# A product-key expert search in which one 128-wide tail search per head replaces two 64-wide ones

## What is computed

```python
h = dct(frames(x))                         # (32, 313, 128)
h = h + attention(layernorm(h))
hid = layernorm(h)
q = layernorm_heads(hid @ Wq.T + bq)       # 8 heads x 64, two halves of 32
s0 = l2norm(q[..., :32]) @ l2norm(keys0).T # 64 scores per head and half
s1 = l2norm(q[..., 32:]) @ l2norm(keys1).T
sc0, ix0 = top_k(s0, 16)
sc1, ix1 = top_k(s1, 16)
cs = sc0[..., :, None] + sc1[..., None, :] # 16 x 16 candidates
ci = ix0[..., :, None] + ix1[..., None, :] # the expert of a candidate (0 to 126)
fs, pos = top_k(cs, 16)
w = softmax(fs)
out = h + sum over heads and picks of gelu(hid . down[fi]) * w * up[fi]
```

## Time and profile before

| | |
|---|---|
| median of 3 runs | 2107.41 us (2103.27 to 2129.34) |
| the profiled execution | 2100.36 us |
| its span (first to last instruction) | 2098.2 us |
| DVE busy | 1929.6 us (92%) |
| PE busy | 1694.7 us (81%) |
| POOL busy | 1634.6 us (78%) |
| ACT busy | 1215.4 us (58%) |
| DMA engines busy | 10% or less in every slice |

### The profile page before, as it was taken

The page is one execution under the profiler, slowest core; times in us unless marked ns, Lnnn a source line. Parts: engine busy times, 40 slices in busy tenths (PEclk is TensorE's granted clock), DMA queues, the critical chain, the costliest instruction groups (busy, mean ns, idle before and its releaser), DMA issues.

```text
span 2098.2 us, 48149 instructions
## 1 busy us (share of the span) xinstructions
PE 1694.7 (81%) x10975; PEld 1316.2 (63%) x10975; DVE 1929.6 (92%) x15878; ACT 1215.4 (58%) x3835; POOL 1634.6 (78%) x3523
## 2 busy tenths in 40 slices
PE   5567898878889887887888788788878988888666
PEld 3335576765767676575767667676766766566555
DVE  3299999999999999999999999999999999999992
ACT  3345655566565566666566666656666566665454
POOL 2238787897878788787878878787887878888785
PEclk9676767778776777887677788767877677776655
DMA  1000000000000000000000000000000000000000
GB/s 35 12 10 2 19 7 7 19 9 18 6 19 7 6 19 9 19 7 19 7 6 18 9 19 7 19 6 6 19 9 19 7 13 13 6 13 9 6 8 9
DMA packets 46676, 24.86 MB, mean 12 GB/s; under 512 B 4955, under 2 KB 46116, under 8 KB 46390
## 3 DMA queue, kind: packets, MB, share of 16 engines
q1 hardware_dynamic: 46390, 21.80, 3.7%
HBM read 11.52 MB, written 10.26 MB: 10 GB/s over the span
## 4 chain that ended last, share of the span: by engine, by line
PE 38%; DVE 30%; POOL 13%; ACT 12%; issue 7%; SPq 0%; another core or an unknown queue 0%; DMA 0%; ACTq 0%; DVEq 0%; POOLq 0%
PE QB L529 7%; DVE alpha L1050 5%; PE FB L447 5%; PE FB L438 5%; PE SC L481 4%; DVE idx L1034 4%; DVE idx L1037 4%; DVE hrest L1028 3%; PE QB L517 3%; PE FB L419 3%; ACT WD L729 3%; POOL sa L759 3%; ACT hi L669 3%; PE FB L427 3%; DVE vals L1032 2%
## 5 line engine op out<-in xcount | busy, mean ns | idle before, releaser
L529 PE MATMUL QB<-bw,alpha 128*128 128x48 bf16 x5120 | 553.8, 277 | 58.0 <-issue 56.8
L529 PEld LDWEIGHTS QB<-bw,alpha 128*128 128x128 bf16 x5120 | 522.1, 151 | 95.5 <-issue 85.9
L896 POOL TENSOR_TENSOR bw<-beta,wp 128x1024 bf16<-128x1024 bf16 x240 | 504.1, 2130 | 96.9 <-ACT wp L715 96.9
L729 ACT ACTIVATE WD<-QB 32x96 f32<-32x96 f32 x1280 | 307.5, 240 | 78.5 <-PE QB L529 67.3
L481 PE MATMUL SC<-WK,hidT 128*128 128x512 f32 x320 | 238.5, 837 | 54.2 <-ACT stdT L661 52.2
L1050 DVE TENSOR_SCALAR alpha<-hi 128x1024 bf16<-128x1024 bf16 x640 | 274.2, 499 | 0.0
L1034 DVE FIND_INDEX8 idx<-vals,sraw 128x8 uint32<-128x64 f32 x1280 | 250.7, 217 | 0.0
L1037 DVE FIND_INDEX8 idx<-vals,hrest 128x8 uint32<-128x64 f32 x1280 | 250.4, 217 | 0.0
L1028 DVE MATCH_REPLACE8 hrest<-vals,sraw 128x64 f32<-128x64 f32 x1280 | 249.9, 208 | 0.0
L838 POOL TENSOR_TENSOR ci<-idxf 128x64 f32<-128x64 f32 (+3 forms) x400 | 123.6, 342 | 119.3 <-DVE beta L1056 119.0
L722 ACT ACTIVATE ofin<-QB 128x128 f32<-128x128 f32 x80 | 22.2, 278 | 287.1 <-PE QB L529 284.5
(11 more groups left out here) (206 smaller groups left out, 4092.4 us busy)
## 6 DMA issues: line engine op xcount, KB each, us to landing
res<-h_scratch SPq DMA_DIRECT2D x80, 64.0 KB, 1.8
xin<-in_x SPq DMA_DIRECT2D x32, 128.0 KB
h_scratch<-h2n SPq DMA_DIRECT2D x32, 128.0 KB
out<-ofin SPq DMA_DIRECT2D x64, 64.0 KB, 1.5
h_scratch<-h2n SPq DMA_DIRECT2D x32, 28.5 KB
out<-ofin SPq DMA_DIRECT2D x16, 57.0 KB
xin<-in_x SPq DMA_DIRECT2D x32, 28.0 KB
xin<-in_x SPq DMA_DIRECT2D x32, 0.2 KB
```

What stands on the lines that cost most here:

```text
L529: last = mm(bank[:, 48 * u:48 * u + 48], alpha[:, buf, a, :, 8 * p + u], bwv[:, :, a, :, 8 * p + u], start=(a == 0), stop=(a == 1))
L729: last = A(WD[r, RING[(t - 4) % NT], :, 8 * p:8 * p + 8], blocks[r, :, :, g], ACT.Copy)
L896: last = tt(bw[:, buf, NY * i:NY * i + NY, :], beta[:, buf, :, :], wp[:, buf, i, :].unsqueeze(1).to_broadcast([128, NY, 256]), ALU.mult)
```

## The change

Only the best 8 of each score group are searched for in the group itself. Of the 9th to 16th of one half, only the sum with the other half's best can be a pick. So, for each head, the rests of both halves lie side by side in `rest` (128 columns); ACT multiplies each half's 64 columns by its inverse norm and adds the best value of the other half (16 instructions in place, bias and scale both a column of the partitions, L718 of the new file). DVE then finds the best 8 of the 128 with one `max` per head, straight into the last 8 cells of `cs`, and one `max_index`. Cells are now 38 in three rectangles and 8 tail cells: 46 for 54, and the first candidate search covers 30 for 44. The expert number of a tail cell is worked out on ACT (four more small instructions) and POOL (four). `Yw` and `Ye` are written by one instruction each, cell-major, and PE folds the rows above 128 with small matmuls onto free rows (`FOLD`). `wexp` moves from p = 0 of one slot to p = 1 of the slot before, the Newton steps of `rn` from p = 0 of t = 0 to p = 1 of the t = 4 before, and both `mark` copies go.

```diff
--- before.py
+++ after.py
@@ -25,13 +25,16 @@
-CAND = [(0, 1, 16, 0), (1, 1, 8, 16), (2, 2, 5, 24), (4, 4, 3, 34), (8, 8, 1, 46)]
-NC = 54
-NC8 = 44
+CAND = [(0, 2, 8, 0), (2, 2, 5, 16), (4, 4, 3, 26)]
+TAILS = 38
+NC = 46
+NC8 = 30
+FOLD = [(slice(32, 36), 0, 4), (slice(38, 40), 1, 8), (slice(40, 44), 1, 4), (slice(44, 46), 0, 12)]
@@ -157,29 +163,35 @@
-        mark = sb("mark", [128, 2 * NT])
-        hrest = sb("hrest", [128, 1024])
-        vals = sb("vals", [128, 3, 16, TOP])
...
+        rest = sb("rest", [128, 1024])
+        vals = sb("vals", [128, 3, 16, 8])
+        first = sb("first", [128, 16])
...
-        wexp = sb("wexp", [128, H, NC])
+        wexp = sb("wexp", [128, 2, H, NC])
...
-        Yw = sb("Yw", [128, 2, H, 32])
-        Ye = sb("Ye", [128, 2, H, 32], BF16)
+        Yw = sb("Yw", [128, NC, H])
+        Ye = sb("Ye", [128, NC, H], BF16)
@@ -485,10 +497,13 @@
                 for a in range(2):
-                    for blk in range(2):
-                        cells = src[:, blk, 4 * a:4 * a + 4, :].rearrange("p h r -> p (h r)")
-                        last = mm(dst[:, 128 * a:128 * a + 128], cells, eye[:], start=(a == 0 and blk == 0),
-                                  stop=(end and a == 1 and blk == 1), skip_group_check=True)
+                    last = mm(dst[:, 128 * a:128 * a + 128], src[:, 16 * a:16 * a + 16, :].rearrange("p c h -> p (c h)"),
+                              eye[:], start=(a == 0), stop=False, skip_group_check=True)
+                for i, (cells, a, row) in enumerate(FOLD):
+                    w = H * (cells.stop - cells.start)
+                    last = mm(dst[8 * row:8 * row + w, 128 * a:128 * a + 128],
+                              src[:, cells, :].rearrange("p c h -> p (c h)"), eye[:], start=False,
+                              stop=(end and i == len(FOLD) - 1), skip_group_check=True)
                 return last
@@ -669,14 +684,11 @@
                 if p == 0 and exists(k, t, 2):
-                    buf = RING[(t - 2) % NT]
                     act.wait_ge(s["c2_full"], n - 1)
                     after(act, s["zs_full"], n - 2)
                     A(zexp[:], top[:], ACT.Exp).then_inc(s["zexp_full"], 1)
                     after(act, s["y_full"], n - 2)
                     A(m[:], c2[:], ACT.Relu, scale=-1.0, bias=cpick[:]).then_inc(s["m_full"], 1)
-                    after(act, s["wz_full"], n - 2)
-                    A(wexp[:], cs[:, buf, :, :], ACT.Exp).then_inc(s["wexp_full"], 1)
@@ -693,7 +705,23 @@
                     buf = RING[(t - 1) % NT]
                     act.wait_ge(s["halves_full"], n)
                     after(act, s["ci_full"], n - 1)
-                    A(idxf[:], idx[:, buf, :, :], ACT.Identity, bias=cquart[:]).then_inc(s["idxf_full"], 1)
+                    A(idxf[:], idx[:, buf, :, :], ACT.Identity, bias=cquart[:])
+                    A(idx0[:], idx[:, buf, 0:16:2, 0], ACT.Identity, bias=cfar[:])
+                    A(tailf[:], idxt[:, buf, :, :], ACT.Identity, bias=cquart[:])
+                    A(tail64[:], idxt[:, buf, :, :], ACT.Identity, bias=cstep[:]).then_inc(s["tails_full"], 1)
+                    act.wait_ge(s["tails_full"], n)
+                    A(tailh[:], tail64[:], ACT.Identity, scale=1.0 / KEYS, bias=cback[:]).then_inc(s["idxf_full"], 1)
+                if p == 1 and exists(k, t, 0):
+                    act.wait_ge(s["first_full"], n + 1)
+                    for i in range(16):
+                        act.wait_ge(s["rest_steps"], 16 * n + i + 1)
+                        last = A(rest[:, KEYS * i:KEYS * i + KEYS], rest[:, KEYS * i:KEYS * i + KEYS], ACT.Identity,
+                                 scale=rn[:, k % 2, 16 * t + i:16 * t + i + 1], bias=first[:, i ^ 1:(i ^ 1) + 1])
+                    last.then_inc(s["rest_full"], 1)
+                if p == 1 and exists(k, t, 1):
+                    act.wait_ge(s["cs_full"], n)
+                    after(act, s["wz_full"], n - 2)
+                    A(wexp[:, (n - 1) % 2, :, :], cs[:, RING[(t - 1) % NT], :, :], ACT.Exp).then_inc(s["wexp_full"], 1)
@@ -860,32 +887,39 @@
-                if p == 0 and t == 0 and exists(k, t, 0):
-                    pool.wait_ge(s["seed4_full"], k + 1)
-                    newton(y4[:], xh4[:], na[:], c15[:], s["rn_steps"], 12 * k, rn[:])
...
-                    cells(ci[:, buf, :, :], idxf[:], s["ci_full"])
+                    second = idxf[:, 1:16:2, 0]
+                    tt(idxd[:], idx0[:], second, ALU.subtract).then_inc(s["idxd_full"], 1)
+                    cells(ci[:, buf, :, :], idxf[:], None)
+                    pool.wait_ge(s["idxd_full"], n)
+                    tt(tailu[:], tailh[:], idxd[:].unsqueeze(2).to_broadcast([128, H, 8]), ALU.mult).then_inc(s["tailu_steps"], 1)
+                    pool.wait_ge(s["tailu_steps"], 2 * n - 1)
+                    tt(tailu[:], tailu[:], tailf[:], ALU.add).then_inc(s["tailu_steps"], 1)
+                    pool.wait_ge(s["tailu_steps"], 2 * n)
+                    tt(ci[:, buf, :, TAILS:NC], tailu[:], second.unsqueeze(2).to_broadcast([128, H, 8]), ALU.add
+                       ).then_inc(s["ci_full"], 1)
+                if p == 1 and t == NT - 1 and exists(k, t, -1):
+                    pool.wait_ge(s["seed4_full"], k + 2)
+                    newton(y4[:], xh4[:], na[:], c15[:], s["rn_steps"], 12 * (k + 1), rn[:, (k + 1) % 2, :])
...
                     for Y, src in ((Yw, wz[:]), (Ye, ci[:, buf, :, :])):
-                        tt(Y[:, 0, :, :], src[:, :, 0:32], m[:, :, 0:32], ALU.mult)
-                        for cell, row in share:
-                            last = tt(Y[:, 1, :, row], src[:, :, cell], m[:, :, cell], ALU.mult)
+                        last = tt(Y[:].rearrange("p c h -> p h c"), src, m[:], ALU.mult)
@@ -1008,34 +1042,35 @@
-                if p == 0 and exists(k, t, 0):
-
-
-                    dve.wait_ge(s["sraw_full"], n + 1)
-                    after(dve, s["cs_full"], n - 1)
-                    after(dve, s["idxf_full"], n - 1)
-                    V.tensor_copy(mark[:, t:t + 1], ident[:, 0:1])
...
+                        dve.wait_ge(chain, 16)
+                        dve.wait_ge(s["rn_steps"], 12 * k + 12)
+                        V.tensor_tensor(first[:], vals[:, buf, :, 0], rn[:, k % 2, 16 * t:16 * t + 16], ALU.mult
+                                        ).then_inc(s["first_full"], 1)
                         for i in range(16):
-                            dve.wait_ge(chain, i + 1)
-                            V.match_replace(rest[i], vals[:, buf, i, 0:8], raw[i], -1e30).then_inc(chain, 1)
+                            V.match_replace(rest[:, KEYS * i:KEYS * i + KEYS], vals[:, buf, i, :], raw[i], -1e30
+                                            ).then_inc(s["rest_steps"], 1)
...
-                            dve.wait_ge(chain, 16 + i + 1)
-                            V.max(vals[:, buf, i, 8:16], rest[i]).then_inc(chain, 1)
-                        for i in range(16):
-                            V.max_index(idx[:, buf, i, 0:8], vals[:, buf, i, 0:8], raw[i]).then_inc(chain, 1)
-                        for i in range(16):
-                            dve.wait_ge(chain, 32 + i + 1)
-                            last = V.max_index(idx[:, buf, i, 8:16], vals[:, buf, i, 8:16], rest[i])
-                            last.then_inc(chain if i < 15 else s["halves_full"], 1)
+                            V.max_index(idx[:, buf, i, :], vals[:, buf, i, :], raw[i]).then_inc(chain, 1)
+                        both = [rest[:, 2 * KEYS * h:2 * KEYS * h + 2 * KEYS] for h in range(H)]
+                        dve.wait_ge(s["rest_full"], n + 1)
+                        after(dve, s["wexp_full"], n - 1)
+                        for h in range(H):
+                            V.max(cs[:, buf, h, TAILS:NC], both[h]).then_inc(chain, 1)
+                        for h in range(H):
+                            dve.wait_ge(chain, 32 + h + 1)
+                            last = V.max_index(idxt[:, buf, h, :], cs[:, buf, h, TAILS:NC], both[h])
+                            last.then_inc(chain if h < H - 1 else s["halves_full"], 1)
@@ -1069,24 +1104,26 @@
                         dve.wait_ge(s["cs_full"], n)
-                        after(dve, s["wexp_full"], n - 1)
-                        V.tensor_copy(mark[:, NT + t:NT + t + 1], ident[:, 0:1])
-                        chain = s["cand_chain"]
...
+                        dve.wait_ge(s["wexp_full"], n)
...
-                            V.match_replace(crest[:, h, :], top[:, h, 0:8], cs[:, buf, h, :], PICKED).then_inc(chain, 1)
+                            V.match_replace(cs[:, buf, h, 0:NC8], top[:, h, 0:8], cs[:, buf, h, 0:NC8], PICKED
+                                            ).then_inc(chain, 1)
...
+                        after(dve, s["m_full"], n - 1)
```

More of the change, by code:

```diff
@@ L838, in cells @@
                     last = tt(o, a0, a1, ALU.add)
[L839 to L844 removed]
+                if done is not None:
```

(1 more changed line is left out.)

56 lines of the change are left out of this document (34 added, 22 removed).

## The result

The changed kernel takes 2416.97 us (median of 4 runs, 2414.89 to 2418.1), the kernel before 2109.01 us on the same chip: ratio 1.1429, 95% interval [1.1374, 1.1484]. Forecast were 2385 us and a range of 2200 to 2480. The profiled executions have spans of 2416.3 and 2098.2 us and mean granted clocks of 0.677 and 0.737. Some executions run slower at a lower granted clock, whatever the kernel, and the ratios leave them out, as two of the eight of e1 (the six others have a median of 2088.8 us).

A forecast was written before the change was run, and what follows sets the result against it. It took an ACT-PE loop (about 119.3 us per pair) beside DVE's (about 119.6) as the bound; ACT's additions lengthen the first by 18.9 us per pair, over 15 pairs 284 us on 2100.4: 2385 us, range 2200 to 2480.

The forecast's parts named there:

- Two loops of nearly equal length: Kernel before: ACT-PE loop about 119.3 us per pair beside DVE's own about 119.6.
- The rule cited: Optimize the engine with highest occupancy; backs the rival that DVE bounds and new ACT work hides: 1952 us, chance 0.07.
- DVE's gain: Smaller searches and index passes save DVE 1.85 us per slot, 148 us over 80 slots; worth nothing in the time.
- ACT's additions: Net 6.0 us more per slot on ACT (4.0 to 7.1), 5.1 of it the sixteen instructions at 0.32 each.
- The index group: ACT's index conversions grow from one start-to-start of some 0.40 us to five: +0.95 us per slot.
- The rival at VectorE's pace: ACT's sixteen run at DVE's pace, 3.1 us: 10.9 us less per pair, 2264 us; chance 0.12.
- The ledger per pair: Start of PE's second `less`: +5.5 (t = 3), +3.9 (4), +3.1 (0), +1.4 (1), +5.0 (2), sum 18.9 us.
- PE's clock: Rival: PE comes back from idle time at the low clock, 6 us more per pair, 2475 us; chance 0.08.
- The row folding: Two more PE matmuls each in EB and U, about 0.9 us per slot, counting at t = 4 and t = 0.
- The total: 15 pairs of 18.9 us, 284 us, on the profiled 2100.4 us: say 2385 us; last pair about unchanged.
- The waits: PE's second `less` waits 3 to 6 us except in t = 1; DVE waits 4 to 8 for `rest`, share 78%.
- where it hurts: ACT's additions stand between `Gd` and `sraw`, ahead of the second `wp`, so PE's second `less` waits for them.

The follow-up runs named there:

- e1: Changed kernel with one of ACT's sixteen `rest` instructions per slot, the other fifteen left out; 2095.48 us, 0.989 of the kernel before.
- e10: Changed kernel with one of sixteen `rest` instructions and, after the first tile, one of ACT's five index instructions; 2070.61 us, 0.9784 of the kernel before.
- e4: Kernel before plus sixteen idle ACT instructions per slot between `Gd` and `sraw`; 2309.21 us, ratio 1.0962.
- e12: Changed kernel with `rest` made by two wide VectorE instructions instead of ACT's sixteen; 2211.81 us, 1.0442 of the kernel before.
- e9: Kernel before with ACT's whole list in a new order, `wp` and its `less` first, no instruction added or removed; 2295.21 us, ratio 1.0902.
- e6: Changed kernel with 24 to 75 useless matmuls on PE ahead of its wait for the second `wp` in four slots; 2392.66 us, 1.1356 of the kernel before.
- e2: Changed kernel with DVE searching unscaled rests, so it does not wait for ACT before the tail search; 2412.73 us, 1.1454 of the kernel before.
- e5: Kernel before plus sixteen idle ACT instructions per slot behind the third `wp` copy; 2260.62 us, ratio 1.0737.
- e7: Changed kernel with ACT's sixteen `rest` instructions moved behind the third `wp` copy; 2483.93 us, 1.1799 of the kernel before.

## Why the prediction was right, and where not

**Two loops of nearly equal length.** Right in what it was used for: with DVE busy 98 to 104 us less and most of ACT's additions gone, the time falls by 23 us (e1) or 46 us (e10), in the profiled executions mostly outside the full pairs; lengthening ACT's side costs 200 us (e4) in a kernel where DVE has the same work. That DVE's loop was just behind is shown by e12: there DVE's time counts, 116 us of 207. The picture of two loops is too simple even so: e9 lengthens no engine's work, only moves it, and costs 190 us, with waits of DVE and POOL that the prediction did not have. The rule cited, to optimize the most occupied engine (the Trainium skill, Perfetto Trace Analysis, section Identifying the Most-Contended Engine), did not lead far here: the engine at 92% was relieved, and even with ACT's sixteen all but gone that gave 1.1% (e1).

**DVE's gain.** 148 us forecast, 135.5 measured here, 98 in e1 and 104 in e10. Eight `max` over 128 columns take 1.65 us busy, 0.195 from start to start (0.188 forecast), and an index pass with its load 0.26 us, as forecast; the tail search is 3.67 us (3.6). The mis-sized term is `first`: put at 0.2 us a slot, it takes 0.48 in the changed kernel and 0.93 in e1, 22 and 58 us more over 80 slots (last section).

```profile
1324.54 1.65 DVE L1069 MAX8 cs<-rest 128x8 f32<-128x128 f32 x8 [4.59 <-ACT rest L718]
...
1326.36 0.08 DVE L1072 MATCH_VALUE_LOAD idxt<-cs,rest 128x8 f32 x1
...
1326.62 0.08 DVE L1072 MATCH_VALUE_LOAD idxt<-cs,rest 128x8 f32 x1
...
1328.21 0.80 DVE L1111 MAX8 top<-cs 128x8 f32<-128x30 f32 x8
```

**ACT's additions.** Right, and their sizes too: 0.332 us each for 0.32, in all 5.42 for 5.1. The estimate of 0.33 by the Trainium skill (ScalarE: Activation LUTs, section What ACT_TABLE_LOAD costs) agrees with the 0.332 of the trace. The index group takes 1314.45 - 1313.08 = 1.37 us from its start to the next instruction where it took about 0.40: +0.97 for a forecast +0.95. `rest` found its inputs ready (4.6 us of idle time in 80 slots). The rival at VectorE's pace (2264 us) fell with that.

**The ledger per pair.** Right in its pattern (least in t = 1, then t = 4, no wait in t = 1), too small in its sum: 23.4 for 18.9 us, most of it in t = 0 (+1.9), t = 2 and t = 3 (+1.3 each). What was mis-sized is PE's clock, which the sum left out and only a rival had (6 us a pair): 1.7 us in t = 3 by the variance blocks above, and some 3 us a pair by the estimate under e6. What remains of the 4.5 us is not assigned.

The row folding was put at 0.9 us a slot, and that was twice too much. At 2.4 GHz EB and U took

```profile
1006.30 0.40 PE L490 MATMUL EB<-identb,Ye 128*128 128x128 bf16 x4
1006.54 1.11 PE L490 MATMUL U<-ident,Yw 128*128 128x128 f32 x8
```

and take now

```profile
1278.96 0.29 PE L500 MATMUL EB<-identb,Ye 128*128 128x128 bf16 x2
1279.18 0.29 PE L504 MATMUL EB<-identb,Ye 128*32 128x128 bf16 x4
1279.40 0.71 PE L500 MATMUL U<-ident,Yw 128*128 128x128 f32 x4
1280.04 0.62 PE L504 MATMUL U<-ident,Yw 128*32 128x128 f32 x8
```

From the first start to the last end that is 1.35 and 1.70 us, +0.35; at 1.2 GHz it is 2.42 and 2.87, +0.45. But in three of five slots of the changed kernel the group runs at 1.2 GHz, 2.79 us in the mean, where the same slots of the kernel before had 1.75 to 2.21: half or more of what it costs there is clock again. POOL lost 2.2 us a slot (178 in 80), as forecast.

**The total.** It came within 1.3%, partly by luck. The change itself is 318 us in the profiled executions where the sum had 284. The full pairs were 56 us dearer than the ledger says. Against that, the sum gave the start 18.9 us, a fifteenth pair, and it cost 9; and it took the end as unchanged, which gained 12.

**The waits.** The second `less` waits in four of five slots as said; 3.2 us in t = 3 and t = 4 were inside 3 to 6, 8.1 us in t = 2 and 6.7 to 8.9 in t = 0 outside. The longest wait was expected in t = 4, where it is the shortest. DVE's wait for `rest` was put at 4 to 8 us a slot and is 233.0 / 74 = 3.1; its share fell to 74%, not 78%; it also waits 188.8 us for `hi`. That the wait for `rest` is without cost was right (e2); the one for `hi` was not taken away in any run. ACT at 70% is as said.

**A step that the outcome hid.** The prediction called it the place "where it hurts" and implied that a place behind the second `less` would hurt less. That holds for idle instructions (e5 under e4 by 49 us), but e7 refutes it for the real ones: the place behind the third `wp` costs 67 us more. The prediction's number didn't rest on it, its lesson did.

## What to carry to other kernels

Before work is moved from one engine to another, compare how long each loop is, not how busy each engine is: an engine at 58% that waits for an engine that waits for it has no room. Price moved work by its time from start to start and expect nearly all of it back in the time once the first slack is gone; and weigh instruction counts, since sixteen narrow ScalarE instructions (5.42 us) did what two wide ones on VectorE did in 2.50 us. A probe with idle instructions (e4, e5) tests one loop only; move the real ones, with those who wait for them, before trusting it. A filler against the clock has to run in the idle time itself: look in the trace whether the work behind it got faster (e6). And read the busy time that a change saves in each version anew: here it was 98 to 135 us for the same instructions of DVE, mostly by what POOL did beside them.
